# Leaky ReLU of the edge loop in two operations of two tiles, and the window sum moved between the two head sums

## The chip, the cores and the metric

The kernel runs on one core of one Trainium2 chip. The time is the device time of one execution in microseconds (us), from one launch to its end. A profiled execution adds a trace: for every instruction its engine, start and duration. The engines are TensorE (PE in the rows, PEld for its weight loads), VectorE (DVE), ScalarE (ACT), GpSimd (POOL) and SyncE (SP). Each has its own instruction queue, in order. They are tied to each other by semaphores alone. A name with a q behind it (DVEq) is an engine's sequencer, which does registers, waits and branches.

## The reference, cut to what matters

The work is a two-layer graph network over 6250 nodes of 128 features and 100,000 edges. The change lies in layer 0:

```
f    = (e @ fc_w.T).reshape(-1, 4, 128)        # 100000 edges, 4 heads
w    = attn[rel]                               # 100 relations
feat = sum over heads of leaky_relu(w * f, 0.2)
msg  = x[src] + feat
x    = layernorm(x + segment_sum(msg, dst))    # edges are sorted by dst
...                                            # then layer 1: attention over the edges sorted by src
```

Layer 1 (a segment softmax and a weighted sum) and the final normalization follow, and the change does not touch them.

## The kernel before, in words

**Edge loop.** The edges of layer 0 are worked in 196 groups (`G0`) of 512 edges, that is of `TG` = 4 tiles with 128 edges each. One pass over all groups is made in this run. The loop is unrolled; slots (`k`, four of them, `SLOTS`) hold what is in flight: the edge features, the gathered node rows `xg`, the relation one-hots.

**What each engine does for a group.**

- TensorE makes `FP` (features times `fc_w`, 128x512 per tile, L896) and `WP` (the relation's attention row, L905), then adds the messages of an earlier group into a window of 64 nodes (`AP`, L915 and L917), and sorts edge numbers into runs (`EP`, L928).
- ScalarE copies `WP` to `w_sb` (L659), makes the one-hots, and copies the runs (L693).
- VectorE makes, in this order: `joh` (L1205), `z` of tile pair 0 = `FP` times `w_sb` (L1224), of the group before `hs` (L1239: heads 0 and 1 plus heads 2 and 3) and `msg` (L1247: the two halves of `hs`), `z` of pair 1, `accT` of the group two back (L1215: the window is added to the node sums; its place comes from a register that L1211 loads), `add_x` of the group before (L1255: `msg` plus the gathered node rows, for 3 of 4 tiles), and `y` (L1231: the larger of 0.2 z and z, all four tiles at once, 128x2048). In the rows `msg` and `xg` are both called `room`, after the buffer they lie in; the shapes tell them apart: 128x512 from `hs` is `msg`, 128x384 is `add_x`.
- GpSimd issues five indirect DMAs for a group: four gathers of 128 rows of x by source node into `xg` (L539, called `room<-in_x,pk`) and one scatter of the sorted runs of the group three back (L550, `sorted_edges<-runs,spot_i`). The first gather of a group waits for `agg_done` (the slot is free once the group four back has been aggregated), the scatter for `r_copied` and for the scatter before it.
- SyncE issues the loads of the edge features and relations.

**Who holds whom.** VectorE's `add_x` waits for `xg_in`, the landing of the group's gathers. TensorE's aggregation waits for `x_added` and, since there is one `AP`, for `acc_done` of the group before. The next products into `FP` wait for `z_done`. ScalarE's copy of the runs (L693, in `compact`) waits for the scatter of the group four back, and behind it in ScalarE's queue stand the copies to `w_sb` that `z` needs.

**Waits of VectorE on itself.** Every operation waits by semaphore for the ones whose results it reads: `z` for `y_done` of the group before (its buffer is read by `y`), `y` for `z_done` of both pairs, `hs` for `y_done`, `msg` for `hs_done`, `add_x` for `msg_ready`.

Behind the edge loop come the node normalization, layer 1 (whose gathers by GpSimd are L583 and L591), and the output.

Of the kernel before, what the change touches and what calls it, by code (L numbers as in the profile page):

```python
# [5 lines left out]
ALU = mybir.AluOpType  # L6
# [50 lines left out]
SLOPE0, SLOPE1, EPS = 0.2, 0.01, 1e-5  # L57
# [15 lines left out]
def build(nc, x, x_t, e, src_pg, dst_pg, dst_g, rel_g, fcT, attn, WT, Wn, b, a1, a1b, a2, a2b, out):  # L73
    with ExitStack() as ctx:
        def sb(name, shape, dt=F32):
            return ctx.enter_context(nc.sbuf_tensor(name, shape, dt))

        def sem(name):
            return ctx.enter_context(nc.semaphore(name))
# [98 lines left out]
        z = sb("z", [P, 2, 2, D4])  # L178
        y = sb("y", [P, 2, 2, D4])
# [153 lines left out]
        z_done = sem("z_done")  # L333
        y_done = sem("y_done")
# [702 lines left out]
        def _(dve):  # L1037
            v = nc.vector
# [162 lines left out]
            def records(g, k, lead):  # L1201

                if not (lead and k < 2):
                    dve.wait_ge(r_done, g - 1)
                v.tensor_tensor(joh[:, k % 2, :, :], iota_row[:, 0:J].rearrange("p (o w) -> p o w", o=1)  # L1205
                                .to_broadcast([P, TG, J]),
                                rank[:, bass.ds(g * TG, TG)].rearrange("p (u o) -> p u o", o=1)
                                .to_broadcast([P, TG, J]), ALU.is_equal).then_inc(joh_ready, 1)

            def accumulate(g, k, lead):  # L1210
                r = dve.value_load(base_rep[0:1, bass.ds(g, 1)], min_val=0, max_val=NP)  # L1211
                dve.wait_ge(agg_done, g + 1)
                if not (lead and k == 0):
                    dve.wait_ge(acc_done, g)
                v.tensor_tensor(accT[:, bass.ds(r, W)], accT[:, bass.ds(r, W)], AP_[:, 0:W],  # L1215
                                ALU.add).then_inc(acc_done, 1)

            def weigh_pair(g, k, lead, h):

                dve.wait_ge(f_done, 2 * g + h + 1)  # L1220
                dve.wait_ge(w_copied, TG * g + 2 * h + 2)
                if not (lead and k == 0):
                    dve.wait_ge(y_done, g)
                v.tensor_tensor(z[:, h, :, :], FP[h][:, :, :], w_sb[:, h, :, :], ALU.mult).then_inc(z_done, 1)  # L1224

            def slope(g, k, lead):

                dve.wait_ge(z_done, 2 * g + 2)
                if not (lead and k == 0):
                    dve.wait_ge(hs_done, g)  # L1230
                v.scalar_tensor_tensor(y[:, :, :, :], z[:, :, :, :], SLOPE0, z[:, :, :, :], ALU.mult,  # L1231
                                       ALU.max).then_inc(y_done, 1)

            def halve(g, k, lead):

                dve.wait_ge(y_done, g + 1)
                if not (lead and k == 0):
                    dve.wait_ge(msg_ready, g)
                v.tensor_tensor(hs[:, :, :], y_all[:, :, 0:D4 // 2], y_all[:, :, D4 // 2:D4],  # L1239
                                ALU.add).then_inc(hs_done, 1)  # L1240

            def finish(g, k, lead):

                dve.wait_ge(hs_done, g + 1)
                if not (lead and k < 2):
                    dve.wait_ge(agg_done, g - 1)
                v.tensor_tensor(msg[:, k % 2, :, :], hs[:, :, 0:P], hs[:, :, P:2 * P],  # L1247
                                ALU.add).then_inc(msg_ready, 1)

            def add_x(g, k, lead):  # L1250

                dve.wait_ge(msg_ready, g + 1)
                dve.wait_ge(xg_in[k], PASS_IN * p + 16 * TG + (g - k) * 16)
                dve.sem_inc(dve_turn, 1)
                v.tensor_tensor(msg[:, k % 2, 0:X_DVE, :], msg[:, k % 2, 0:X_DVE, :], xg[:, k, 0:X_DVE, 0:P],  # L1255
                                ALU.add).then_inc(x_added, 1)

            def group(g, k, lead):
                prev = None if lead and k == 0 else (g - 1, (k - 1) % SLOTS, lead)
                records(g, k, lead)  # L1260
                weigh_pair(g, k, lead, 0)
                if prev:
                    halve(*prev)
                    finish(*prev)
                weigh_pair(g, k, lead, 1)
                if not (lead and k < 2):
                    accumulate(g - 2, (k - 2) % SLOTS, lead)
                if prev:
                    add_x(*prev)
                slope(g, k, lead)  # L1270

            with dve.Fori(0, pass_count(dve)) as p:
                for k in range(SLOTS):
                    group(k, k, True)
                for g in range(SLOTS, G0):
                    group(g, g % SLOTS, False)
                halve(G0 - 1, SLOTS - 1, False)
                finish(G0 - 1, SLOTS - 1, False)
                add_x(G0 - 1, SLOTS - 1, False)
                accumulate(G0 - 2, SLOTS - 2, False)  # L1280

                dve.wait_ge(gap_made, G0)
                v.tensor_scalar(dloc[:, :], dloc[:, :], float(W), None, ALU.subtract).then_inc(win_step, 1)
                dve.wait_ge(joh_ready, G0)
                v.tensor_scalar(rank[:, :], rank[:, :], float(J), None, ALU.add).then_inc(win_step, 1)
                v.tensor_scalar(spot[:, :], spot[:, :], float(J), None, ALU.subtract).then_inc(win_step, 1)
                v.tensor_scalar(left[:, :], left[:, :], float(J), None, ALU.add).then_inc(win_step, 1)
                dve.wait_ge(win_step, 7 * p + 4)
                v.scalar_tensor_tensor(spot_m[:, :], left[:, :], 0.0, spot[:, :], ALU.is_gt,
                                       ALU.mult).then_inc(win_step, 1)  # L1290
                accumulate(G0 - 1, SLOTS - 1, False)
                dve.wait_ge(acc_done, G0)
                v.tensor_scalar(base_rep, base_rep, W, NP, ALU.add, ALU.min).then_inc(win_step, 1)
                dve.wait_ge(win_step, 7 * p + 6)
                for k in range(SLOTS):
                    dve.wait_ge(sc_in[k], PASS_SC * (p + 1))
                    dve.sem_inc(dve_turn, 1)
                v.tensor_scalar(spot_i[:, :], spot_m[:, :], trash[:, 0:1], None, ALU.add).then_inc(win_step, 1)
                dve.wait_ge(win_step, 7 * p + 7)
                meet(dve, p)  # L1300
# [235 lines left out]
            for j in range(TAIL):  # L1536
                k = j % S1
# [82 lines left out]
```

## Time and profile before

| what | us |
|---|---|
| time, median of 3 runs | 2626.28 |
| lowest and highest of the 3 | 2620.51, 2626.96 |
| span of the profiled execution | 2618.1 |
| edge loop in it, first to last `joh` (195 periods) | 82.80 to 1480.86, 1398.06 in all, 7.17 each |

The span runs from the first to the last instruction; the run's time has some 8 us around it. The profile gives, for the whole span, PE 82% busy, DVE 86%, ACT 66% and POOL 73%. Those are means over two very different halves: in the edge loop VectorE is busy nearly all the time, and in layer 1 all the engines wait more. A timeline row reads: start, duration, engine, line, operation, output <- inputs with their shapes, and in brackets how long the engine was idle before it and what ended that.

### The profile page before, as it was taken

Reading aid. Unit: us, or ns where it says so; the run is one execution under the profiler, and the core shown is the slowest. Engines: PE = TensorE matmul, PEld = TensorE weight load, DVE = VectorE, ACT = ScalarE, POOL = GpSimd, SP = SyncE. Lnnn points to the kernel's source line nnn. Section 1 sums busy time; section 2 is a strip of 40 time slices with the busy share of each in tenths; the row PEclk is TensorE's granted clock in tenths of the full one; section 3 lists DMA queues with packets and bytes.
Section 4 is the critical chain, followed back from the end, with each engine's and each line's share of the span. In section 5 each row is a group of like instructions: output and inputs, shape, how many; then the busy total and the mean of one; then the engine's idle time right before and its main releaser. Section 6 shows DMA issues by size and latency. Waiting matters only on the chain.

```text
span 2618.1 us, 44445 instructions
## 1 busy us (share of the span) xinstructions
PE 2159.8 (82%) x11261; PEld 1538.3 (59%) x11261; DVE 2255.1 (86%) x5754; ACT 1740.7 (66%) x4973; POOL 1919.3 (73%) x1845
## 2 busy tenths in 40 slices
PE   6999999999999999999999846665666666666664
PEld 3566666666666666666666535565656565556554
DVE  9999999999999999999999976666666666677887
ACT  5888888888888888888888644444444444444446
POOL 2487777777777777777777647777777777777773
PEclk8999999999999999999999877777677767777776
DMA  4233333333333333333333233333333333333343
GB/s 133 78 100 104 104 104 103 106 103 102 103 103 105 104 105 105 103 103 102 103 104 104 65 95 81 80 80 80 81 81 80 81 81 82 79 81 79 80 80 80
DMA packets 156600, 244.04 MB, mean 93 GB/s; under 512 B 40836, under 2 KB 84398, under 8 KB 156226
## 3 DMA queue, kind: packets, MB, share of 16 engines
q1 hardware_dynamic: 97730, 132.55, 17.9%
q0 software_dynamic: 58624, 108.72, 17.5%
q8 instruction: 92, 1.51, 0.2%
q14 instruction: 154, 1.26, 0.2%
HBM read 231.99 MB, written 9.12 MB: 92 GB/s over the span
## 4 chain that ended last, share of the span: by engine, by line
DVE 36%; issue 25%; POOL 18%; PE 7%; DMA 6%; DVEq 5%; ACT 1%; POOLq 0%; SPq 0%; ACTq 0%
POOL room L583 17%; DVE y L1231 17%; DVE hs L1239 9%; DMA room<-h_rows,y 5%; DVEq L1211 4%; DVE room L1255 4%; PE FP L986 3%; DVE accT L1215 2%; PE FP L1007 2%; PE AP L1007 1%; DVE z L1224 1%; DMA room<-h_rows,idx 1%; DVE joh L1205 1%; POOL room L591 1%; DVE room L1247 1%
## 5 line engine op out<-in xcount | busy, mean ns | idle before, releaser
L539 POOL DMA_INDIRECT room<-in_x,pk x784 | 920.7, 1174 | 262.5 <-issue 251.0
L583 POOL DMA_INDIRECT room<-h_rows,y x756 | 714.7, 945 | 235.2 <-issue 216.0
L896 PE MATMUL FP<-fc_sb,room 128*128 128x512 f32 x1568 | 832.3, 612 | 2.2 <-issue 2.2
L905 PE MATMUL WP<-at_p,rel_oh 100*128 100x512 f32 x1568 | 803.5, 594 | 0.0
L986 PE MATMUL FP<-ident,room 128*128 128x128 f32 x1664 | 342.7, 370 | 385.9 <-DMA room<-h_rows,y 351.7
L659 ACT ACTIVATE w_sb<-WP 128x512 f32<-128x512 f32 x784 | 464.1, 592 | 225.0 <-PE WP L905 219.7
L986 PEld LDWEIGHTS FP<-ident,room 128*128 128x128 f32 x1664 | 291.0, 263 | 433.3 <-DMA room<-h_rows,y 387.1
L757 ACT ACTIVATE accT<-accT,neg_big 128x512 f32<-128x512 bf16 x208 | 150.0, 722 | 559.6 <-DVE accT L1377 559.6
L905 PEld LDWEIGHTS WP<-at_p,rel_oh 100*128 100x128 f32 x1568 | 297.8, 190 | 376.5 <-issue 376.5
L1224 DVE TENSOR_TENSOR z<-FP,w_sb 128x1024 f32<-128x1024 f32 x392 | 478.6, 1221 | 1.6 <-ACT w_sb L659 1.0
L1231 DVE SCALAR_TENSOR_TENSOR y<-z 128x2048 f32<-128x2048 f32 x196 | 452.4, 2308 | 0.0
L896 PEld LDWEIGHTS FP<-fc_sb,room 128*128 128x128 f32 x1568 | 266.3, 189 | 43.1 <-issue 2.6
L776 ACT ACTIVATE room<-room,pr 128x129 f32<-128x129 f32 x832 | 266.6, 392 | 6.8
L550 POOL DMA_INDIRECT sorted_edges<-runs,spot_i x196 | 190.4, 972 | 90.6 <-issue 60.5
L666 ACT ACTIVATE boh<-arena,rank_pay 128x52 f32<-128x52 bf16 x784 | 239.8, 378 | 0.0
L1239 DVE TENSOR_TENSOR hs<-y 128x1024 f32<-128x1024 f32 x196 | 238.3, 1216 | 0.0
L915 PEld LDWEIGHTS AP<-doh,room 128*128 128x128 f32 x1568 | 190.6, 192 | 54.1 <-DVE room L1255 54.1
L915 PE MATMUL AP<-doh,room 128*128 128x64 f32 x1568 | 211.9, 278 | 6.8 <-DVE accT L1215 3.9
L676 ACT ACTIVATE dot<-iota_row,dloc 128x64 bf16<-128x64 f32 x784 | 206.3, 336 | 0.0
L1387 DVE SCALAR_TENSOR_TENSOR arena<-arena,decay,AP 128x129 f32 x104 | 36.2, 348 | 175.5 <-PE AP L1007 158.9
L1420 DVE CUSTOM_DVE_ANT_0 hs<-accT,FP 128x512 f32<-128x512 f32 x208 | 142.0, 683 | 17.8 <-PE FP L986 11.8
L1387 DVE SCALAR_TENSOR_TENSOR arena<-arena,decay,FP 128x129 f32 x104 | 36.0, 347 | 124.8 <-PE FP L1007 108.2
(246 smaller groups left out, 3181.6 us busy)
## 6 DMA issues: line engine op xcount, KB each, us to landing
room<-in_e SPq DMA_DIRECT2D x196, 256.0 KB, 2.7
rel_sb<-in_rel_g SPq DMA_DIRECT2D x196, 200.0 KB
z<-sorted_sources SPq DMA_DIRECT2D x208, 128.0 KB, 3.0
room<-in_x,pk POOLq DMA_INDIRECT x784
room<-h_rows,y POOLq DMA_INDIRECT x756
sorted_edges<-runs,spot_i POOLq DMA_INDIRECT x196, 2.0
accT<-in_x_t SPq DMA_DIRECT2D x1, 3125.0 KB, 11.2
h_rows<-arena SPq DMA_DIRECT2D x13, 227.5 KB, 2.8
```

What stands on the lines that cost most here:

```text
L539: pool.indirect_dma_start(xg[:, k, u, 0:P], None, x[:, :], bass.IndirectOffsetOnAxis(ap=pk[:, g, u:u + 1], axis=0)).then_inc(xg_in[k], 16)
L583: pool.indirect_dma_start(hg[k][:, u, :], None, h_dram[:, :], bass.IndirectOffsetOnAxis(ap=sd[:, g * TG + u:g * TG + u + 1], axis=0)).then ...
L659: nc.scalar.activation(w_sb[:, u // 2, u % 2, :], WP[u % 2][:, :], ACT.Copy).then_inc(w_copied, 1)
L666: ins = nc.scalar.activation(boh[:, k % 2, u, :], onehot[:, :, bass.ds(g * TG + u, 1)].rearrange("p b o -> p (b o)"), ACT.Identity, bias=0 ...
L776: nc.scalar.activation(hg[k][:, u, 0:P + 1], hg[k][:, u, 0:P + 1], ACT.Identity, bias=0.0, scale=pr[:, k % 2, u:u + 1]).then_inc(h_scaled, 1)
L896: mm = pe.matmul(FP[u // 2][:, u % 2, :], e_sb[:, k, u, :], fc_sb[:, :], start=True, stop=True)
L905: mm = pe.matmul(WP[u % 2][:, :], rel_oh[:, k % 2, u * P:(u + 1) * P], at_p[:, j, :], start=(j == 0), stop=(j == 1))
L915: pe.matmul(AP_[:, 0:W], msg[:, k % 2, u, :], doh[:, k % 2, u, :], start=(u == 0), stop=False)
L986: mm = pe.matmul(rows_of(k)[:, u * P:(u + 1) * P], hg[k][:, u, P + 1:P + 2].to_broadcast([P, P]), ident[:, :], start=True, stop=True)
L1224: v.tensor_tensor(z[:, h, :, :], FP[h][:, :, :], w_sb[:, h, :, :], ALU.mult).then_inc(z_done, 1)
L1231: v.scalar_tensor_tensor(y[:, :, :, :], z[:, :, :, :], SLOPE0, z[:, :, :, :], ALU.mult, ALU.max).then_inc(y_done, 1)
L1239: v.tensor_tensor(hs[:, :, :], y_all[:, :, 0:D4 // 2], y_all[:, :, D4 // 2:D4], ALU.add).then_inc(hs_done, 1)
```

## The change

Two edits to VectorE's queue in the edge loop, and the counts of one semaphore that follow from them.

1. `slope(g)` (one operation on 128x2048) becomes `slope_pair(g, h)` (128x1024), called for both pairs at the end of the group. `y_done` now counts two per group.
2. `accumulate(g - 2)` moves ahead: from behind the second `z` to between `hs` and `msg` of the group before. Its register load (L1211) moves with it.

```
@@ weigh_pair
-                    dve.wait_ge(y_done, g)
+                    dve.wait_ge(y_done, 2 * g - 1 + h)
...
-            def slope(g, k, lead):
+            def slope_pair(g, k, lead, h):
-                dve.wait_ge(z_done, 2 * g + 2)
+                dve.wait_ge(z_done, 2 * g + h + 1)
...
-                v.scalar_tensor_tensor(y[:, :, :, :], z[:, :, :, :], SLOPE0, z[:, :, :, :], ALU.mult,
+                v.scalar_tensor_tensor(y[:, h, :, :], z[:, h, :, :], SLOPE0, z[:, h, :, :], ALU.mult,
                                        ALU.max).then_inc(y_done, 1)
             def halve(g, k, lead):
-                dve.wait_ge(y_done, g + 1)
+                dve.wait_ge(y_done, 2 * g + 2)
...
@@ group
                 weigh_pair(g, k, lead, 0)
                 if prev:
                     halve(*prev)
-                    finish(*prev)
-                weigh_pair(g, k, lead, 1)
                 if not (lead and k < 2):
                     accumulate(g - 2, (k - 2) % SLOTS, lead)
                 if prev:
+                    finish(*prev)
+                weigh_pair(g, k, lead, 1)
+                if prev:
                     add_x(*prev)
-                slope(g, k, lead)
+                slope_pair(g, k, lead, 0)
+                slope_pair(g, k, lead, 1)
```

VectorE's queue for one group in the middle of the edge loop, from `hs` to the next `hs`, before:

```order
L1239 TENSOR_TENSOR hs<-y 128x1024
L1247 TENSOR_TENSOR room<-hs 128x512
L1224 TENSOR_TENSOR z<-FP,w_sb 128x1024
L1211 TENSOR_LOAD win_rep
L1211 ISA x2
L1215 ISA
L1215 TENSOR_TENSOR accT<-accT,AP 128x64
L1255 TENSOR_TENSOR room<-room 128x384
L1231 SCALAR_TENSOR_TENSOR y<-z 128x2048
L1205 TENSOR_TENSOR joh<-iota_row,rank_pay 128x128
L1224 TENSOR_TENSOR z<-FP,w_sb 128x1024
L1239 TENSOR_TENSOR hs<-y 128x1024
```

and the same stretch of the changed kernel:

```order
L1239 TENSOR_TENSOR hs<-y 128x1024
L1211 TENSOR_LOAD win_rep
L1211 ISA x2
L1215 ISA
L1215 TENSOR_TENSOR accT<-accT,AP 128x64
L1247 TENSOR_TENSOR room<-hs 128x512
L1224 TENSOR_TENSOR z<-FP,w_sb 128x1024
L1255 TENSOR_TENSOR room<-room 128x384
L1231 SCALAR_TENSOR_TENSOR y<-z 128x1024 x2
L1205 TENSOR_TENSOR joh<-iota_row,rank_pay 128x128
L1224 TENSOR_TENSOR z<-FP,w_sb 128x1024
```

The load and the sum to `accT` went up by two operations, and `y` is two rows of half the size. GpSimd's queue in the edge loop is the same in both kernels; two groups of it, with the semaphores each waits for:

```order
L539 DMA room<-in_x,pk 128x128 [waits agg_done]
L539 DMA room<-in_x,pk 128x128 x3
L550 DMA sorted_edges<-runs,spot_i 263808x1 [waits r_copied,sc_in2]
L539 DMA room<-in_x,pk 128x128 [waits agg_done]
L539 DMA room<-in_x,pk 128x128 x3
```

Nothing moved there: five issues a group, four gathers and a scatter.

## Rows read from the trace of the kernel before

**Rows 1.** Page, first line: span of the profiled execution.

```profile
span 2618.1 us, 44445 instructions
```

**Rows 2.** Lines of DVE, 400 to 1300 us: busy, mean ns | idle before.

```profile
L1224 DVE TENSOR_TENSOR z<-FP,w_sb 128x1024 f32<-128x1024 f32 x251 | 306.5, 1221 | 0.3 <-issue 0.3
L1231 DVE SCALAR_TENSOR_TENSOR y<-z 128x2048 f32<-128x2048 f32 x126 | 290.7, 2307 | 0.0
L1247 DVE TENSOR_TENSOR room<-hs 128x512 f32<-128x512 f32 x126 | 87.2, 692 | 4.3
```

**Rows 3.** Timeline from 602.7 us, one group, VectorE and GpSimd: start, duration.

```profile
603.31 0.98 POOL L539 DMA_INDIRECT room<-in_x,pk  x1 [0.30 <-issue]
603.32 2.31 DVE L1231 SCALAR_TENSOR_TENSOR y<-z 128x2048 f32<-128x2048 f32 x1
...
604.60 1.86 POOL L539 DMA_INDIRECT room<-in_x,pk  x1 [0.30 <-issue]
...
605.56 0.28 DVE L1205 TENSOR_TENSOR joh<-iota_row,rank_pay 128x128 f32<-128x128 f32 x1
605.77 1.23 DVE L1224 TENSOR_TENSOR z<-FP,w_sb 128x1024 f32<-128x1024 f32 x1
...
606.76 0.94 POOL L539 DMA_INDIRECT room<-in_x,pk  x1 [0.31 <-issue]
...
606.91 1.22 DVE L1239 TENSOR_TENSOR hs<-y 128x1024 f32<-128x1024 f32 x1
...
608.00 0.94 POOL L539 DMA_INDIRECT room<-in_x,pk  x1 [0.30 <-issue]
...
608.16 0.69 DVE L1247 TENSOR_TENSOR room<-hs 128x512 f32<-128x512 f32 x1
...
608.77 1.22 DVE L1224 TENSOR_TENSOR z<-FP,w_sb 128x1024 f32<-128x1024 f32 x1
...
609.25 0.92 POOL L550 DMA_INDIRECT sorted_edges<-runs,spot_i  x1 [0.30 <-issue]
...
609.90 0.21 DVE L1215 TENSOR_TENSOR accT<-accT,AP 128x64 f32 x1
...
610.03 0.55 DVE L1255 TENSOR_TENSOR room<-room 128x384 f32<-128x384 f32 x1
...
610.48 0.98 POOL L539 DMA_INDIRECT room<-in_x,pk  x1 [0.30 <-issue]
610.50 2.31 DVE L1231 SCALAR_TENSOR_TENSOR y<-z 128x2048 f32<-128x2048 f32 x1
```

**Rows 4.** Timeline at 151.1 us: a gather that starts just behind `y`.

```profile
151.11 2.35 DVE L1231 SCALAR_TENSOR_TENSOR y<-z 128x2048 f32<-128x2048 f32 x1
151.13 0.94 POOL L539 DMA_INDIRECT room<-in_x,pk  x1 [0.30 <-issue]
```

**Rows 5.** Timeline at 158.3 us, one group later: the same gather.

```profile
158.32 2.29 DVE L1231 SCALAR_TENSOR_TENSOR y<-z 128x2048 f32<-128x2048 f32 x1
158.35 3.08 POOL L539 DMA_INDIRECT room<-in_x,pk  x1 [0.30 <-issue]
```

**Rows 6.** Timeline from 95.7 us: the first gathers of the loop's steady part.

```profile
95.73 0.29 DVE L1205 TENSOR_TENSOR joh<-iota_row,rank_pay 128x128 f32<-128x128 f32 x1
...
95.81 1.07 POOL L539 DMA_INDIRECT room<-in_x,pk  x1 [8.76 <-PE AP L917]
...
97.09 1.22 DVE L1239 TENSOR_TENSOR hs<-y 128x1024 f32<-128x1024 f32 x1
...
97.19 1.94 POOL L539 DMA_INDIRECT room<-in_x,pk  x1 [0.30 <-issue]
```

**Rows 7.** Timeline at 42.8 us, ahead of the loop: a short two-input operation.

```profile
42.80 0.29 DVE L1148 CUSTOM_DVE_ANT_0 dot<-b_rep,a_rep 128x128 f32<-128x128 f32 x1
42.88 1.03 POOL L539 DMA_INDIRECT room<-in_x,pk  x1 [0.30 <-issue]
```

**Rows 8.** Waits of POOL, 40 to 1500 us: us, times, longest.

```profile
POOL sorted_edges L550 <- ACT runs L693: 27.9, 2, 25.9
POOL room L539 <- PE AP L917: 8.8, 1, 8.8
```

## The prediction

> **What bounds the kernel now.** I read the span first (2618.1 us [rows 1]), then the lines of VectorE in the middle of the edge loop. There VectorE never waits: `z` has 0.3 us of idle time ahead of 251 operations, `y` none; `msg` has 4.3 us ahead of 126, 0.034 each, which is the time from the end of `hs` to the start of `msg`, its reader [rows 2]. So the period of a group, 7.17 us (1398.06 us over 195), is VectorE's own work. In the timeline of one group [rows 3] every VectorE operation but `msg` starts 0.07 to 0.09 us before the one ahead of it ends (z at 605.77 runs to 607.00, hs starts at 606.91); I call this overlap 0.08. The eight durations sum to 7.70; less seven overlaps of 0.08, plus 0.034, that is 7.17. The sum closes.
>
> The reader should now look at the other engine of the same rows. GpSimd never shows a gap longer than 0.31 us, yet its period is the same 7.17. It isn't held by a semaphore: its gate from TensorE (L917) ended a wait once in the whole loop, that of the run copy twice [rows 8]. An engine with five issues of 0.92 to 0.98 us and 0.30 between them would need 5 x 0.94 + 0.04 + 5 x 0.305 = 6.25 us. The missing 0.92 is in one issue, that at 604.60: 1.86 us long, where its like take 0.94. It ends 0.83 after the end of `y` (603.32 + 2.31 = 605.63; 606.46) [rows 3].
>
> **A rule out of five places.** Say a GpSimd issue needs something of VectorE's at about 0.13 us after its start.
>
> - It starts 0.02 after the start of `y`: it passes (0.94), and `y` is stretched to 2.35 [rows 4].
> - It starts 0.03 after: it takes 3.08, and ends 0.82 after `y`, which now takes 2.29 [rows 5].
> - It starts 0.10 after the start of `hs`: 1.94, ends 0.82 after `hs` [rows 6].
> - It starts 0.08 after `joh`, an operation of only 0.29: 1.07, ends 0.86 after it [rows 6]. The like with another short operation with two inputs in SBUF: 1.03, ends 0.82 after it [rows 7].
> - During `z` and the sum to `accT`, which read one input from PSUM, it passes: the scatter at 609.25 takes 0.92 [rows 3].
>
> So an operation that reads two inputs from SBUF (`joh`, `hs`, `msg`, `add_x`, `y`) holds off an issue that starts more than 0.02 us behind its start; the issue then runs 0.82 past its end. The Trainium skill says so too: GPSIMD Engine Reference, section "Key points", has GpSimd share its SBUF interfaces with VectorE, with contention for VectorE instructions with two SBUF inputs. It gives no price; the trace has one.
>
> In the steady part exactly one issue in five is held, by `y`. From the end of `y`, the four issues behind the held one follow freely, and the first gather of the next group starts 4.85 us later (610.48 less 605.63), while the next `y` starts 4.87 later (610.50): 0.02 ahead of `y`, so it passes [rows 3]. That is a narrow place, 0.04 wide by [rows 4, 5], and the change moves `y`.
>
> **The change part by part: VectorE.**
>
> - `accT` between `hs` and `msg`: the wait of 0.034 is covered by accT's 0.21, and one more pair overlaps: 0.034 + 0.08 = 0.114 us less per group. The register load moves with it; it stood behind `z` of 1.22 us, now behind `hs` of 1.22, so its cover is the same. `agg_done` of the group two back is no new wait: the sum now comes some 2.2 us earlier, and TensorE's L917 for it ended in the period before. Behind `accT` stand `msg`, `z` and `add_x`; none of them is late.
> - `y` in two: `y` without disturbance takes 2.29 [rows 5]; `hs` has 1024 columns and takes 1.216 (row 1.22 [rows 3]), and twice the columns would be 2.28, so a half is taken as 1.22. Two, less one overlap: 2.36, against 2.307 now [rows 2]: 0.05 more. From both sides: 0.05 if the 0.02 by which GpSimd now stretches `y` goes away, 0.09 if it comes back in a half.
> - `z` of pair 0 no longer waits for all of `y`; `joh` covered that, so nothing.
>
> VectorE's own period would be 7.17 - 0.114 + 0.05 = 7.11, over 196 groups 12 us less. With the upper bound for the halves, 5 us less. This would be the result if nothing else moved.
>
> **The change part by part: GpSimd.** Count from the end of the second half of `y`. Now the first half starts at 4.87 - 0.114 = 4.75, and the first gather still arrives at 4.85: 0.10 behind it. It is held, by the rule, as it was 0.10 behind `hs` [rows 6]. The first half ends at 5.97, the gather at 6.83 (0.86, first of a group), the next issue starts at 7.13. `joh` stands at 7.03 to 7.31: held by 0.10 behind its start, ends 8.13; next issue 8.43. `hs` stands at 8.37 to 9.59: 0.06 behind, held, ends 10.41; next 10.71, in `z`, free, ends 11.65; next 11.96, and the first half stands at 11.86: held again. So four issues fit in VectorE's 7.11 us, where a group needs five. GpSimd falls 1.8 us behind per group (7.11 / 4 x 5 = 8.88). It can fall behind by no more than the four slots, 4 x 7.17 = 28.7 us, and less by what it has used; so after some 5 to 15 groups VectorE has to wait for it: over `add_x` (landing of gathers), or earlier over ScalarE, whose copy of the runs waits for the scatter of the group four back and has the `w_sb` copies of the next `z` behind it.
>
> When VectorE waits, it holds nothing, and GpSimd runs free in that time. So the period settles between 8.88 and GpSimd's least. The first half holds one issue for 1.0 us (1.94 against 0.94), joh one for 0.10: 6.25 + 1.0 + 0.1 = 7.35. Each group in which `hs` holds one too costs 1.0 more, 8.38. Which of the two comes about hangs on where VectorE's wait falls, and on the landing times, which vary from group to group. I take `hs` in one group in five, since the 0.06 us by which it is hit here is near the 0.02 that passes, and a VectorE that waits comes later: 7.35 + 0.21 = 7.56.
>
> Sum: ten groups at -0.06, 186 at 7.56 - 7.17 = +0.39: -1 + 72 = **+71 us**, a span of 2689 and a time of 2697 us (2626.28 + 71). Against 2618.1 + 8 around it the median is the same. Bounds for this case: `hs` never, +33 (2659); `hs` in half the groups, +0.68 x 186 = +126 (2752); three in five, +145 (2771).
>
> **Rivals.**
>
> 1. *VectorE stays the bound, GpSimd slips in.* If `joh` or `hs` lets the issue pass (0.02 to 0.04 us decide it: a half of 1.25 instead of 1.22, or a boundary between the two halves that leaves more room), five issues fit: one held by the first half, the rest free. Then the VectorE sum holds: -5 to -12 us, 2614 to 2621. For it: the margins are small. Against it: `joh` did hold an issue in [rows 6], and 0.03 was enough to be held in [rows 5].
> 2. *Halfway.* GpSimd passes at `joh` in part of the groups, or loses its place and VectorE waits only now and then; gain and loss cancel within 8 us, 2618 to 2634. It decides itself from about one group in five at 7.35, the others at 7.11.
> 3. *The boundary is shut.* The second half takes over from the first without letting GpSimd in: the gather is held until the end of the second, 3.08 us as in [rows 5]. That is one issue with +2.1: 8.35 per group, less what VectorE's waits give back; up to 2840. Against it: at the end of `y`, `joh` starts 0.07 us before, and the issue held by `y` still ends 0.83 after `y`, not after `joh` [rows 3].
> 4. *The change doesn't do what it says*: `accT` in its new place waits (for its register or for TensorE). Even 0.1 us per group would be 20 us. The load takes its turn behind `hs` as it did behind `z`, so I give it almost nothing.
>
> **How the numbers follow.** Slower by GpSimd's holds 0.70; boundary shut or more holds than I count (over 2771) 0.06; halfway 0.11; VectorE-bound gain 0.13. A measurement of this kernel can tell 0.3%, 8 us, from no change. Slower by more than that: 0.70 + 0.05 = 0.75; within: 0.12; faster: 0.13 (most of the -5 to -12 lies at its far end). The likeliest case's own range is 2655 to 2775. It holds some 0.68, so the range has to reach down over the halfway case and into the gain: 2616 to 2775.
>
> **What the profile of the changed kernel would show.** The two rows of `y` at 1.22 us each, start to start 1.14; no idle time ahead of `msg`; `accT` directly behind `hs`. If I am right on GpSimd: issues of 1.9 to 2.0 us (start behind the first half or `hs`) and of 1.05 (behind `joh`), more than one held issue per group; and VectorE's `z` or `add_x` with idle time, tens of us in all, released by ScalarE's `w_sb` or by the gathers; ScalarE's L693 waiting for the scatter. If rival 1 holds, VectorE has no idle time, the period is 7.11, and one issue of 1.9 us stands in each group. I'd be wrong at the root if GpSimd's long issues no longer ended 0.82 behind an operation with two SBUF inputs.

## The result, and the profile after

The changed kernel takes 2756.99 us (median of 4 runs, 2754.8 to 2760.34). The kernel before, timed beside it, takes 2624.86 (2620.51 to 2626.96, 4 runs). The ratio is 1.0507 with a 95% interval of 1.0492 to 1.0522: 132 us slower. I had forecast +71 us, with 2616 to 2775 as the range.

The first lines of the page of the changed kernel: span, then busy time, share and instructions of each engine.

```profile
span 2753.0 us, 44836 instructions
PE 2207.8 (80%) x11261; PEld 1540.5 (56%) x11261; DVE 2257.2 (82%) x5950; ACT 1700.6 (62%) x4973; POOL 2057.0 (75%) x1845
```

VectorE is as busy as before, in microseconds (2257.2 against 2255.1), while the span went from 2618.1 [rows 1] to 2753.0. So in sum VectorE's work got no dearer; idle time was added. GpSimd's busy time is what grew, from 1919.3 to 2057.0 us, with the same 1845 instructions. The groups of the page show where it grew, and who waits (line, engine, operation, count | busy us, mean ns | idle before, and what ended most of it):

```profile
L539 POOL DMA_INDIRECT room<-in_x,pk x784 | 1028.6, 1312 | 262.4 <-issue 249.5
L1224 DVE TENSOR_TENSOR z<-FP,w_sb 128x1024 f32<-128x1024 f32 x392 | 478.4, 1220 | 126.1 <-issue 123.3
L1231 DVE SCALAR_TENSOR_TENSOR y<-z 128x1024 f32<-128x1024 f32 x392 | 461.3, 1218 | 0.0
L550 POOL DMA_INDIRECT sorted_edges<-runs,spot_i x196 | 221.1, 1128 | 92.6 <-issue 62.9
L693 ACT ACTIVATE runs<-EP 52x32 f32<-52x32 f32 x196 | 37.1, 189 | 343.7 <-DMA sorted_edges<-runs,spot_i 343.6
```

The mean gather was 1174 ns before and is 1312 now, the mean scatter 972 and now 1128: 784 x 0.138 + 196 x 0.156 = 139 us more of GpSimd. And there are two new waits. VectorE's `z` (0.3 us of idle time in [rows 2], over 900 us) has 126 us. ScalarE's copy of the runs, L693, waits 343.6 us for the scatter; before, its waits between 95 and 1640 us name no scatter. The half of `y` takes 1218 ns, as estimated.

From first to last `joh` the edge loop runs from 82.79 to 1609.19 us, 1526.4, that is 7.83 per group against 7.17: +128.3 us. The 6.6 us left of the span's +134.9 lie behind the last `joh`: from its start to the end of the span it is 1143.8 us, against 1137.2 before.

Besides `z`, only `add_x` has a wait of some size, for its gathers. From the waits of 95 to 1640 us (who waited for what: us, times, longest):

```profile
DVE room L1255 <- DMA room<-in_x,pk: 11.2, 16, 1.8
```

The "issue" beside `z` hides the cause, as a `z` waits for several semaphores. The timeline shows it. First the time in which GpSimd falls behind: one group from 134 us on, VectorE and GpSimd (start us, us, engine, line; "x2" is both halves of `y` as one row):

```profile
134.03 1.22 DVE L1239 TENSOR_TENSOR hs<-y 128x1024 f32<-128x1024 f32 x1
134.14 1.92 POOL L539 DMA_INDIRECT room<-in_x,pk  x1 [0.30 <-issue]
...
136.37 0.94 POOL L539 DMA_INDIRECT room<-in_x,pk  x1 [0.30 <-issue]
...
137.50 2.35 DVE L1231 SCALAR_TENSOR_TENSOR y<-z 128x1024 f32<-128x1024 f32 x2
137.62 1.92 POOL L539 DMA_INDIRECT room<-in_x,pk  x1 [0.30 <-issue]
...
139.77 0.28 DVE L1205 TENSOR_TENSOR joh<-iota_row,rank_pay 128x128 f32<-128x128 f32 x1
139.84 1.01 POOL L550 DMA_INDIRECT sorted_edges<-runs,spot_i  x1 [0.30 <-issue]
...
141.10 1.22 DVE L1239 TENSOR_TENSOR hs<-y 128x1024 f32<-128x1024 f32 x1
141.16 2.02 POOL L539 DMA_INDIRECT room<-in_x,pk  x1 [0.30 <-issue]
```

VectorE has no idle time here: `hs` to `hs` is 141.10 - 134.03 = 7.07 us, less than the 7.17 of before. In that time GpSimd starts four issues, at 134.14, 136.37, 137.62 and 139.84, where a group needs five. Three of the four start just behind the start of an operation with two SBUF inputs and end 0.80 to 0.82 behind its end: the gather at 134.14 ends at 136.06 (`hs` ended at 135.25), the one at 137.62 ends at 139.54 (the first half of `y` ended near 138.72), the scatter at 139.84 ends at 140.85 (`joh` ended at 140.05).

Once the loop is in step, `z` of VectorE waits for the first time at 190.34. That is some 13 groups behind the first held gathers at 97 us and 8 behind the group shown. From there on the loop looks like this; the rows are of VectorE, GpSimd and ScalarE, 1000 us in:

```profile
1002.42 1.22 DVE L1239 TENSOR_TENSOR hs<-y 128x1024 f32<-128x1024 f32 x1
...
1002.88 1.56 POOL L550 DMA_INDIRECT sorted_edges<-runs,spot_i  x1 [0.30 <-issue]
...
1006.07 0.19 ACT L693 ACTIVATE runs<-EP 52x32 f32<-52x32 f32 x1 [2.32 <-DMA sorted_edges<-runs,spot_i]
...
1009.38 1.23 DVE L1224 TENSOR_TENSOR z<-FP,w_sb 128x1024 f32<-128x1024 f32 x1 [0.43 <-issue]
```

The scatter starts 0.46 us behind `hs`, ends 0.80 behind its end, and lands later; ScalarE has waited 2.32 us for it at 1006.07. Behind L693 in ScalarE's queue stand the one-hots (1.22 us at 1006.16), a copy to `w_sb`, `dot` (1.06) and the second copy of the pair (0.59 at 1008.71). Only then can `z` start, at 1009.38. That is the wait of 0.43 us that the row puts down to "issue".

### The profile page after: what moved, and what is told of

Same layout as the page of the kernel before. It is cut to its first block and busy times, and to the rows that moved or that the text cites. A ratio compares the mean times of both kernels' runs of the same rounds, so it can differ in the third digit from the quotient of the medians.

```text
span 2753.0 us, 44836 instructions
## 1 busy us (share of the span) xinstructions
PE 2207.8 (80%) x11261; PEld 1540.5 (56%) x11261; DVE 2257.2 (82%) x5950; ACT 1700.6 (62%) x4973; POOL 2057.0 (75%) x1845
## 5 line engine op out<-in xcount | busy, mean ns | idle before, releaser
L539 POOL DMA_INDIRECT room<-in_x,pk x784 | 1028.6, 1312 | 262.4 <-issue 249.5
L896 PE MATMUL FP<-fc_sb,room 128*128 128x512 f32 x1568 | 832.3, 612 | 12.5 <-DVE z L1224 7.0
L905 PE MATMUL WP<-at_p,rel_oh 100*128 100x512 f32 x1568 | 771.1, 573 | 15.9 <-ACT w_sb L659 15.9
L905 PEld LDWEIGHTS WP<-at_p,rel_oh 100*128 100x128 f32 x1568 | 291.2, 190 | 413.4 <-issue 290.6
L659 ACT ACTIVATE w_sb<-WP 128x512 f32<-128x512 f32 x784 | 457.0, 583 | 52.9 <-PE WP L905 52.3
L1231 DVE SCALAR_TENSOR_TENSOR y<-z 128x1024 f32<-128x1024 f32 x392 | 461.3, 1218 | 0.0
L896 PEld LDWEIGHTS FP<-fc_sb,room 128*128 128x128 f32 x1568 | 267.1, 190 | 57.2 <-issue 17.8
L550 POOL DMA_INDIRECT sorted_edges<-runs,spot_i x196 | 221.1, 1128 | 92.6 <-issue 62.9
L915 PEld LDWEIGHTS AP<-doh,room 128*128 128x128 f32 x1568 | 194.2, 192 | 135.9 <-DVE room L1255 129.7
L915 PE MATMUL AP<-doh,room 128*128 128x64 f32 x1568 | 212.8, 279 | 69.9 <-DVE room L1255 64.4
L693 ACT ACTIVATE runs<-EP 52x32 f32<-52x32 f32 x196 | 37.1, 189 | 343.7 <-DMA sorted_edges<-runs,spot_i 343.6
```

The source lines that it names most:

```text
L539: pool.indirect_dma_start(xg[:, k, u, 0:P], None, x[:, :], bass.IndirectOffsetOnAxis(ap=pk[:, g, u:u + 1], axis=0)).then_inc(xg_in[k], 16)
L659: nc.scalar.activation(w_sb[:, u // 2, u % 2, :], WP[u % 2][:, :], ACT.Copy).then_inc(w_copied, 1)
L896: mm = pe.matmul(FP[u // 2][:, u % 2, :], e_sb[:, k, u, :], fc_sb[:, :], start=True, stop=True)
L905: mm = pe.matmul(WP[u % 2][:, :], rel_oh[:, k % 2, u * P:(u + 1) * P], at_p[:, j, :], start=(j == 0), stop=(j == 1))
L915: pe.matmul(AP_[:, 0:W], msg[:, k % 2, u, :], doh[:, k % 2, u, :], start=(u == 0), stop=False)
L1231: v.scalar_tensor_tensor(y[:, h, :, :], z[:, h, :, :], SLOPE0, z[:, h, :, :], ALU.mult, ALU.max).then_inc(y_done, 1)
```

## Experiments

Each ratio is against the runs of the kernel before that ran beside the kernel in question. Their median was 2624.86 us for the changed kernel, 2620.6 for the first set of experiments (`e1`, `e2`, `e3`, `e6`) and 2621.59 for the second (`e4`, `e7`, `e8`, `e9`). The changed kernel was not timed again beside them, so a difference from its 2756.99 us is good to some 4 us. The period is the time from first to last `joh` divided by 195.

| kernel | us | ratio (95%) | period |
|---|---|---|---|
| before | 2620.6 | 1 | 7.17 |
| after | 2756.99 | 1.0507 (1.0492 to 1.0522) | 7.83 |
| e1_split | 2633.45 | 1.0048 (1.0032 to 1.0063) | 7.24 |
| e2_acc | 2863.19 | 1.0921 (1.0905 to 1.0938) | 8.36 |
| e3_pause | 2659.8 | 1.0149 (1.0133 to 1.0164) | 7.38 |
| e6_order | 2863.44 | 1.0931 (1.0916 to 1.0945) | 8.42 |
| e4_three_after | 2609.9 | 0.9958 (0.9942 to 0.9973) | 7.11 |
| e7_three_acc | 2611.25 | 0.9959 (0.9944 to 0.9975) | 7.11 |
| e8_spread | 2639.7 | 1.0067 (1.0054 to 1.0081) | 7.26 |
| e9_joh | 2608.04 | 0.9948 (0.9935 to 0.9962) | 7.11 |

**The theory** is that of the prediction: GpSimd's issues are held by VectorE's operations with two SBUF inputs, and whoever moves those by a tenth of a microsecond decides how many issues of a group are held. The rivals have letters in the expectations. Rival A: having `y` in two operations is dear by itself. Rival B: the window sum (`accT`) waits in its new place. Rival C: only VectorE's own account counts. Besides these, the loss could come from memory traffic, that is from how late the DMAs land and not from how late they are issued.

### Each half of the change alone

`e1_split` leaves `accT` where it was and splits `y`. Against the changed kernel:

```
                 if prev:
                     halve(*prev)
+                    finish(*prev)
+                weigh_pair(g, k, lead, 1)
                 if not (lead and k < 2):
                     accumulate(g - 2, (k - 2) % SLOTS, lead)
-                if prev:
-                    finish(*prev)
-                weigh_pair(g, k, lead, 1)
                 if prev:
                     add_x(*prev)
```

> The change's first half alone: y in two operations, accT where it was before. Theory (GpSimd's issues are held by VectorE operations with two SBUF inputs): the first half of y starts 4.87 us after the end of the one before, as y did, so the first gather (4.85) still passes; one issue per group is held, by the second half, GpSimd keeps up, and only VectorE's own work counts: two halves of 1.22 less one overlap of 0.08 are 2.36 against 2.29, +0.07 per group, +14 us: about 2639. Rival A (the loss of the changed kernel comes from having y in two operations, however placed: more instructions, more semaphore traffic): most of the +132 us is here, about 2740. Rival B (the loss comes from the new place of accT, whose wait or register load holds up msg): 2639 here too, so this run doesn't tell B from the theory.

Measured: 2633.45 us, 13 more than before. The timeline at 1000 us:

```profile
1000.03 2.40 DVE L1231 SCALAR_TENSOR_TENSOR y<-z 128x1024 f32<-128x1024 f32 x2
1000.04 0.98 POOL L539 DMA_INDIRECT room<-in_x,pk  x1 [0.30 <-issue]
...
1001.33 1.92 POOL L539 DMA_INDIRECT room<-in_x,pk  x1 [0.30 <-issue]
```

The first gather still passes, 0.01 behind the start of the first half, and stretches it. The second is held by the second half and takes 1.92 us, about as much as the 1.86 that it took behind the whole `y` [rows 3]. So GpSimd's row has one held issue a group, as before, and the 0.07 us by which the period grew is the price of the halves themselves (two starts, and the stretch).

`e2_acc` leaves `y` whole and moves `accT`. Against the kernel before:

```
                 if prev:
                     halve(*prev)
+                if not (lead and k < 2):
+                    accumulate(g - 2, (k - 2) % SLOTS, lead)
+                if prev:
                     finish(*prev)
                 weigh_pair(g, k, lead, 1)
-                if not (lead and k < 2):
-                    accumulate(g - 2, (k - 2) % SLOTS, lead)
```

> The change's second half alone: accT between hs and msg, y in one operation. Theory: y starts 0.11 us earlier after the one before, so the first gather arrives 0.10 behind its start and is held for all of it (3.08 us, as in the row at 158.35 of before); four issues instead of five per period, GpSimd falls behind until ScalarE waits for the scatter: 7.8 us per group, +120 us, about 2745, at least +30. Rival C (VectorE's own account, in which the move saves 0.114 us per group): -22 us, 2603. Rival A: no loss here. Rival B: most of the +132 here, but then with idle time ahead of accT or msg, where the theory has none.

Measured: 2863.19 us, 243 more than before and 106 more than the whole change. The lines of VectorE, 400 to 1300 us (as above; the last number is idle time ahead):

```profile
L1224 DVE TENSOR_TENSOR z<-FP,w_sb 128x1024 f32<-128x1024 f32 x212 | 259.0, 1222 | 105.2 <-ACT w_sb L659 102.9 <-issue 2.1
...
L1247 DVE TENSOR_TENSOR room<-hs 128x512 f32<-128x512 f32 x107 | 73.3, 685 | 0.0
L1255 DVE TENSOR_TENSOR room<-room 128x384 f32<-128x384 f32 x106 | 59.0, 557 | 35.1 <-DMA room<-in_x,pk 34.7
...
L1215 DVE TENSOR_TENSOR accT<-accT,AP 128x64 f32 x107 | 23.0, 215 | 0.0
```

There is no idle time ahead of `accT` in its new place, nor ahead of `msg`. So rival B is out. The idle time is ahead of `z`, which waits for ScalarE's copies, and ahead of `add_x`, which waits for its gathers. And the timeline has the cause (columns as in the timelines above):

```profile
1005.45 2.28 DVE L1231 SCALAR_TENSOR_TENSOR y<-z 128x2048 f32<-128x2048 f32 x1
...
1005.70 2.85 POOL L539 DMA_INDIRECT room<-in_x,pk  x1 [0.30 <-issue]
```

This gather starts 0.25 us behind the start of a whole `y` and takes 1.9 us more than a free one; behind a half it was 1.0 us more.

I matched each issue between 400 and 1500 us (130 groups, period 8.48) with the operation whose end it follows by 0.8 us. Beside 6.25 us of free issues, a group has 1.66 us of hold behind `y`, 0.54 behind `hs` and 0.03 behind `add_x`: 8.48 in sum.

My expectation had the direction and the cause, but only half of the loss, and its 7.8 us per group doesn't follow from its own premise. A gather held for all of `y` (3.08 us) is 2.14 us longer than a free one, so the period would have been 6.25 + 2.14 = 8.39. That this is near the measured 8.36 is luck: `y` holds for less on average (1.66), and the hold by `hs` (0.54) was left out. So the loss comes with the move of `accT`, which shortens VectorE's own work. Splitting `y` costs 13 us by itself, and gives back 106 once `accT` has moved. The effects of the two halves, +13 and +243, don't add up to +132.

### Fewer issues for GpSimd

`e4_three_after` has VectorE's queue as in the changed kernel, but only three gathers per group (behind the first four groups); for the fourth tile the rows from the first groups stay in place. The gather of every fourth tile is left out. (The constant for the landings of a whole pass changes with it and isn't shown.)

```
-                for u in range(TG):
+                for u in range(TG if lead else TG - 1):
...
-                dve.wait_ge(xg_in[k], PASS_IN * p + 16 * TG + (g - k) * 16)
+                dve.wait_ge(xg_in[k], PASS_IN * p + 16 * TG + (g - k) * 12)
```

> The changed kernel with three gathers per group instead of four behind the first four groups: the gather of every fourth tile's node rows is left out (old rows of that tile are used). VectorE's, ScalarE's and TensorE's queues are as in the changed kernel. Theory (five issues don't fit between VectorE's two-input operations, four do): GpSimd keeps up, the wait of ScalarE for the scatter and VectorE's idle time are gone, 7.10 us per group, -13 us against before: about 2608, 150 us faster than the changed kernel. Rival A (y in two) and B (accT's place): the loss stays, about 2755; less DMA traffic could give some us back, no more. With landing times as the cause (DMA queues too slow, not the issue), part of it, 2680 to 2740.

Measured: 2609.9 us, as expected. Three of its four issues are held, just as in the changed kernel, but four are all it has:

```profile
1003.24 2.35 DVE L1231 SCALAR_TENSOR_TENSOR y<-z 128x1024 f32<-128x1024 f32 x2
1003.35 1.92 POOL L539 DMA_INDIRECT room<-in_x,pk  x1 [0.30 <-issue]
...
1005.51 0.28 DVE L1205 TENSOR_TENSOR joh<-iota_row,rank_pay 128x128 f32<-128x128 f32 x1
1005.58 1.01 POOL L550 DMA_INDIRECT sorted_edges<-runs,spot_i  x1 [0.30 <-PE AP L917]
...
1006.85 1.21 DVE L1239 TENSOR_TENSOR hs<-y 128x1024 f32<-128x1024 f32 x1
1006.89 2.02 POOL L539 DMA_INDIRECT room<-in_x,pk  x1 [0.30 <-issue]
```

These are nearly the margins of the prediction (0.11 behind the first half, 0.07 behind `joh`, 0.04 behind `hs`), and the holds it gave them. VectorE's `z` has 0.0 us of idle time from 400 to 1300 us. So the whole loss of the change is that GpSimd can't place its fifth issue; no cost of the change's own is left. It also rules out rivals A and B, for which the loss should have stayed. Less traffic and earlier landings are part of this run too; `e3_pause` below tells them apart. That the period is just 7.11, VectorE's forecast, is less of a proof than it looks, as the next run shows.

`e7_three_acc` is the same with the `accT` move alone (its `y` is whole).

> accT moved alone, y in one operation, with the same three gathers per group (every fourth tile's gather left out). Theory: the +240 us of accT moved alone are gone altogether; GpSimd's four issues fit, and VectorE saves 0.114 us of wait and overlap and the 0.02 by which GpSimd stretched y: 7.03 us per group, -27 us against before, 2594. This is what the move of accT is worth to VectorE by itself. Rival B (accT in its new place waits): above 2640.

Measured: 2611.25 us. The 243 us are gone, as the theory has it. But the period should have been 7.03 us (2594 us in all) and is 7.11, like that of `e4_three_after`, though VectorE has less to do. The time missing is at the second `z` of a group. VectorE and ScalarE:

```profile
1002.76 0.60 ACT L659 ACTIVATE w_sb<-WP 128x512 f32<-128x512 f32 x1 [0.42 <-PE WP L905]
...
1002.76 0.68 DVE L1247 TENSOR_TENSOR room<-hs 128x512 f32<-128x512 f32 x1
1003.45 1.22 DVE L1224 TENSOR_TENSOR z<-FP,w_sb 128x1024 f32<-128x1024 f32 x1
```

`z` starts just as `msg` ends, and not 0.08 earlier as in the kernel before. Over 400 to 1300 us the overlap of these two is 0.001 us on average, where it was 0.083 before: a wait of 0.08 us per group that no column of idle time shows. What `z` waits for is ScalarE's copy, which ends at 1003.36 and had waited 0.42 us for TensorE's L905 itself. The chain of work that ended last between 1000 and 1008 us has the same (start, us, what), first its shares by line:

```profile
by line: PE FP L896 57.5%; PE WP L905 23.2%; PE AP L915 10.5%; PE EP L928 6.3%; PE AP L917 4.2%
...
1000.02 0.91 PE FP L896 x2
...
1007.13 0.91 PE FP L896 x2
```

All of it is TensorE, 7.11 us from one group's first products to the next's. In the kernel before, the same view of the same stretch is led by VectorE's `y` (L1231) with 55.6%, and no line of TensorE is in it. So TensorE is next behind VectorE, by 0.06 us a group. While TensorE's work stays as it is, an order of VectorE's queue can be worth some 12 us in this loop and no more; none of the orders tried here got past that.

`e4_three_after` shows the same in small: there `z` overlaps `msg` by 0.046 us on average, so it too waits, by some 0.04 us per group. Without this VectorE's own period would be about 7.07 (an estimate: 7.11 less 0.04), and the group of the changed kernel shown from 134.03 on, in which VectorE has no wait, took just that.

### More work for VectorE

`e3_pause` adds two small memsets of an unused place in `stats` ahead of the first half. They write SBUF and read nothing. From start to start they take 0.16 and 0.10 us, and `add_x` overlaps the first of them by 0.02 us, where it overlaps `y` by 0.08 without them: 0.31 us more for VectorE in each group.

```
                     add_x(*prev)
+                v.memset(stats[:, 0:24, :], 0.0)
+                v.memset(stats[:, 24:48, :], 0.0)
                 slope_pair(g, k, lead, 0)
```

> The changed kernel with two small memsets of unused memory (122x144 each) on VectorE between add_x and the first half of y: more work, nothing computed with it. Theory: the first half starts 0.1 to 0.3 us later, so the first gather gets in ahead of it again; one or two held issues per group, GpSimd keeps up, and the period is VectorE's 7.11 plus the memsets, 7.2 to 7.4: 2640 to 2675, some 80 to 115 us FASTER than the changed kernel. Rivals A and B: the added work can only cost, 2757 or up to 60 us more.

Measured: 2659.8 us, 97 less than the changed kernel, with more to compute. The timeline shows what the pause does:

```profile
1002.03 0.94 POOL L539 DMA_INDIRECT room<-in_x,pk  x1 [0.30 <-issue]
1002.09 0.18 DVE L1272 MEMSET stats<- 122x144 f32 x1
1002.19 2.35 DVE L1231 SCALAR_TENSOR_TENSOR y<-z 128x1024 f32<-128x1024 f32 x2
1003.27 0.94 POOL L539 DMA_INDIRECT room<-in_x,pk  x1 [0.30 <-issue]
...
1005.79 1.21 DVE L1239 TENSOR_TENSOR hs<-y 128x1024 f32<-128x1024 f32 x1
1005.84 2.02 POOL L539 DMA_INDIRECT room<-in_x,pk  x1 [0.30 <-issue]
```

A gather starts 0.16 ahead of the first half and passes. The next starts 0.06 ahead of the second half and 0.14 before the first one ends; it takes 0.94 us like a free one, so it is not held either. What is left is the issue behind `hs` and the short hold by `joh`. Between 200 and 1500 us these are 1.02 and 0.06 us per group, so GpSimd needs 6.25 + 1.02 + 0.06 = 7.33 us and keeps up. The period is 7.38, VectorE's own 7.07 (the estimate above) with the 0.31 of the pause. A kernel that gets 97 us faster by 0.31 us more work in each group isn't bound by VectorE's work, and its memory traffic, the same in both, isn't the reason for the loss.

### A better order

Three orders were tried that keep the change and should let GpSimd pass.

`e6_order` works hs, the first half of `y`, the second `z`, `msg`, the second half, `add_x`, `accT`, so that each half of `y` stands apart.

> Another order of the same nine operations, with y in two: joh, z of pair 0, hs, first half of y, z of pair 1, msg, second half of y, add_x, accT. Theory: hs to msg has work between, so VectorE's own account is that of the changed kernel, 7.10 us per group; and between the two-input operations there is twice a z of 1.22 us in which GpSimd's issues pass, so that no more than one or two in a group are held and five fit. 7.10 against 7.17: -13 us, 2612, faster than both kernels. Rival A: above 2700, as y is in two here too. If the order asks more of TensorE and ScalarE than I see (z of pair 1 waits for its products), VectorE gets idle time ahead of z and the time is 2620 to 2660.

Measured: 2863.44 us, a miss by 251. By the number alone this would fit rival A (above 2700), and it would fit holds of GpSimd. The waits of 200 to 1500 us (who waited for what: us, times, longest) say otherwise:

```profile
ACT w_sb L659 <- PE WP L905: 365.3, 424, 2.1
...
PE AP L915 <- DVE accT L1215: 168.0, 154, 1.4
DVE z L1224 <- ACT w_sb L659: 164.3, 154, 1.4
```

With `add_x` and `accT` at the end of VectorE's group, TensorE's aggregation (L915) waits for `accT`; behind it in TensorE's queue stand the next products (L896, L905), behind these ScalarE's copy to `w_sb`, and behind that the second `z`, which stands ahead of the next `add_x` and `accT`. So the waits form a ring. It takes 8.42 us (second `z` at 1003.68 and 1012.10). GpSimd isn't behind in it: it waits for TensorE itself, 239.7 us in this stretch (L539 for L917). So the reading from the waits is that `accT` has to come early enough for TensorE, and this bounds where it may stand. Rival A is ruled out by `e8_spread` and `e9_joh`, which have `y` in two as well and lose 18 us or nothing.

`e8_spread` mends that: hs, first half of `y`, `msg`, second `z`, `accT`, `add_x`, second half.

> The nine operations in another order: joh, z of pair 0, hs, first half of y, msg, z of pair 1, accT, add_x, second half of y. Against the order of e6, add_x and accT come right behind the second z again. Theory: TensorE's aggregation waits for add_x and accT, and the products behind it end 4.7 us later in the copy that the second z needs; from the start of that z to the end of add_x are now 1.8 us, so this ring is 6.6 us and bounds nothing. The first half of y covers hs to msg. GpSimd has two issues held or fewer. 7.10 us per group, -13 us, 2608: faster than before. Rival (the ring is longer than I count, or three holds in a group): 2630 or more.

Measured: 2639.7 us, again a miss, by 32. The first half of `y` writes over what `hs` reads, so it can start only when `hs` is done:

```profile
L1231 DVE SCALAR_TENSOR_TENSOR y<-z 128x1024 f32<-128x1024 f32 x248 | 302.8, 1221 | 13.6 <-DVE hs L1239 0.9
```

13.6 us of idle time in 124 groups is 0.11 each, and with the overlap of 0.08 that is lost there, 0.19. With VectorE's own 7.07 (the estimate above) this makes 7.26, and 7.26 was measured.

`e9_joh` only exchanges two neighbours of the changed kernel: `joh` goes behind the first `z`.

```
+                weigh_pair(g, k, lead, 0)
                 records(g, k, lead)
-                weigh_pair(g, k, lead, 0)
```

> The changed kernel with one line moved: joh behind the first z instead of ahead of it. Theory: in the changed kernel the issue released at the end of the first half of y ran into joh 0.07 us behind its start, and the next one into hs. With joh behind z, the issues have z of 1.22 us right behind y: the next one passes there, and the one after comes at 2.4, behind the start of hs or joh by one hold at most. Five fit; 7.12 us per group, -10 us, 2611, some 145 us faster than the changed kernel for a move of one short operation. Rivals A and B: no effect, 2755.

Measured: 2608.04 us, a hit, 13 us faster than before and 149 faster than the changed kernel. Its timeline:

```profile
1005.17 2.35 DVE L1231 SCALAR_TENSOR_TENSOR y<-z 128x1024 f32<-128x1024 f32 x2
1005.41 1.80 POOL L539 DMA_INDIRECT room<-in_x,pk  x1 [0.30 <-issue]
1007.44 1.22 DVE L1224 TENSOR_TENSOR z<-FP,w_sb 128x1024 f32<-128x1024 f32 x1
1007.51 0.94 POOL L539 DMA_INDIRECT room<-in_x,pk  x1 [0.30 <-PE AP L917]
1008.58 0.28 DVE L1205 TENSOR_TENSOR joh<-iota_row,rank_pay 128x128 f32<-128x128 f32 x1
...
1008.76 0.93 POOL L550 DMA_INDIRECT sorted_edges<-runs,spot_i  x1 [0.30 <-issue]
1008.78 1.24 DVE L1239 TENSOR_TENSOR hs<-y 128x1024 f32<-128x1024 f32 x1
```

The gather held by the first half ends at 1007.21, and the next starts at 1007.51, 0.07 behind the start of `z`. That is the place where `joh` stood. `z` has one input in PSUM and doesn't hold it, so it takes 0.94 instead of 1.01 to 1.03, and the scatter after it starts at 1008.76, 0.02 ahead of `hs` instead of just behind it, and with `joh` nearly over. It takes 0.93 us, like a free one. One held issue in five is left (the row at 1005.41), and the period is 7.11, where TensorE stands too.

## Why the prediction was right in its mechanism and short in its size

**The rule and the first groups: right.** The prediction put the first gather 0.10 behind the first half, `joh` hit by 0.10 and `hs` by 0.06. The trace after shows 0.12, 0.07 and 0.06, the holds 1.92, 1.01 and 2.02 us, and four issues in 7.07 us. The lag reaches VectorE after 13 groups, within the 5 to 15 given. The waits are those named: L693 for the scatter, `z` behind ScalarE, `add_x` now and then for its gathers. Issues of 1.1 us or more that started by an operation with two SBUF inputs ended 0.78 to 0.87 us behind it, in all ten kernels.

The Trainium skill (GPSIMD Engine Reference, section "Key points") names contention on the SBUF interfaces with VectorE instructions that have two SBUF inputs. The traces agree: each hold shown here is behind such an operation, and behind `z`, with one input in PSUM, the gather of `e9_joh` took 0.94.

The edge of 0.02 us in the rule isn't sharp. An issue 0.024 behind `y` was held ([rows 5], the row at 158.35), while in the changed kernel one 0.042 behind `add_x`, at 257.58, took 0.94. The prediction needed 0.06 or more, so nothing hung on this.

**VectorE's own account: near, and its exact number is luck.** 7.11 us was forecast, and `e4_three_after`, which has the same queue, runs at 7.11 with no idle time ahead of `z`. But this 7.11 is TensorE's, which was not seen; VectorE's own would be about 7.07. The halves take 1.218 (1.22 forecast). Part of the 0.04 is the term that was put at nothing because `joh` covered it: `z` behind `joh` overlaps it by 0.081 us in `e4_three_after`, by 0.066 before.

**The boundary between the halves (rival 3) is open,** as the prediction took to be likelier. A gather held by the first half ends 0.82 behind that half, not behind the second (137.62 above). **The new place of `accT` (rival 4) has no wait.** Its idle time is 0.0. **VectorE stays the bound (rival 1)** doesn't occur here, but `e9_joh` is that case brought about by hand. **Halfway (rival 2)** doesn't occur either: `joh` holds an issue in 95% of the groups.

**The step that failed is the share of `hs`.** I took `hs` to hold a gather in one group of five, for 1.0 us, which makes 0.21 per group. I matched every issue of the changed kernel between 200 and 1600 us (887 in 176 groups) with the operation whose end it follows by 0.8 us. Per group, the rows below the first being what the hold adds:

| held by | forecast us | measured us | measured share of groups |
|---|---|---|---|
| free issues, all five | 6.25 | 6.25 | |
| first half of `y` | 1.0 | 0.87 | 0.97 |
| second half | 0 | 0.05 | |
| `joh` | 0.10 | 0.08 | 0.95 |
| `hs` | 0.21 | 0.65 | 0.97 |
| sum | 7.56 | 7.90 | |

The period in that stretch is 7.89. The missing 0.34 is `hs` with 0.44 too little, and the other terms together with 0.10 too much.

My reason for one in five was that a VectorE that waits comes later and lets the gather ahead of `hs`. What the waiting does is shift `hs` against the issues by a part of its length. Of the 170 issues held by `hs`, a quarter start less than 0.08 us behind its start and are held for all of it; half start more than 0.39 behind. Such a one is the scatter at 1002.88: 0.46 behind the start, 1.56 us long, 0.6 more than a free one. So `hs` is hit nearly always, but mostly in part. The forecast had only whole hits of 1.0 and misses of 0.

With the measured holds in its sum the forecast is 186 x (7.90 - 7.17) = 136 us, and +132 was measured. With the `hs` term alone put right it is 186 x (8.00 - 7.17) = 154, as the first half was taken 0.13 too dear.

The bound that I gave for this term, three groups in five, was 2771, and the result lies below it. That is luck: the share was 0.97, and with whole hits in so many groups the time would have been some 2845 (an estimate: 7.35 + 0.97 x 1.03 = 8.35 us per group). It is below only because most hits are partial, which the forecast didn't have.

**Smaller points.** The 6.6 us by which the time behind the last `joh` grew were not in the sum. `accT` comes 1.86 us earlier behind the start of `hs` (1.13 instead of 2.99), not 2.2 as the prediction says. The 8 us said to lie around the span compare it with the median of other executions: the execution with the span of 2753.0 took 2754.8, so 1.8 us lie around it. Neither touches the +71. ScalarE's wait is longer than the held issue makes it, as the scatter also takes longer to land. The page's list of issues (queue, count, median us from issue to landing) has, after:

```profile
sorted_edges<-runs,spot_i POOLq DMA_INDIRECT x196, 3.7
```

It was 2.0 before. Why it lands later is open. A later landing doesn't cost by itself: in `e9_joh` the median is 2.9, and there is no loss. A landing as late as 3.7 without the held issues wasn't tried.

## What to carry to other kernels

An engine that never shows a wait can still be timed by another: look for one whose period equals the bound's while its own instructions sum to less, and find the instruction that is too long and whose end it follows. Where GpSimd issues DMAs beside a tuned VectorE queue, as here, each issue should start beside a VectorE operation with an input in PSUM, or just ahead of one with two SBUF inputs. In this kernel a tenth of a microsecond decided, and exchanging two neighbours was worth more than the change itself. Idle time alone doesn't show every wait: compare also how far neighbours overlap. Test such a theory by taking an issue away or by adding work: if more work makes the kernel faster, the account of busy time isn't what bounds it.

## What the runs showed that I had not expected

- Hidden behind VectorE stands TensorE, which needs 7.11 us per group, against VectorE's 7.17. Three quite different kernels (`e4_three_after`, `e7_three_acc`, `e9_joh`) end there, at 7.105 to 7.112.
- 0.31 us more of VectorE's work per group made the changed kernel 97 us faster. The memsets of 122x144 take 0.18 us each.
- A large VectorE operation in one piece is the worst neighbour: in `e2_acc` issues held by a whole `y` take 2.60 us on average and up to 3.07, in the changed kernel those held by a half at most 1.97. Yet the whole `y` did no harm in the kernel before, since there one gather passed ahead of it and the next came when more than half of it was over [rows 3].
- Here an operation that overwrites what its neighbour reads waits as one does that reads what its neighbour writes: 0.19 us per group for `y` behind `hs`, against the 0.114 that `msg` behind `hs` was worth in the kernel before.
